# Masked attention: contiguous query operands, first scores between output projections, reciprocals through transposes, pieces in thirds, beginning reordered

## The reference

```python
x = x + _L0_xattn_ref(_layernorm(x, axis=-1), ctx_2048, mask_SxS2_bc0, mask_BxS2_bk0, ...)   # this one
x = x + _L0_ffn_ref(...)
x = x + _L1_xattn_ref(...)
x = x + _L1_ffn_ref(...)

def _L0_xattn_ref(X, encoder_output, causal_mask, padding_mask, Wq, bq, Wk, bk, Wv, bv, Wo, bo):
    q = X @ Wq.T + bq; k = encoder_output @ Wk.T + bk; v = encoder_output @ Wv.T + bv
    scores = einsum('bgrqd,bgkd->bgrqk', q, k) / sqrt(16)
    scores = where(causal_mask, -inf, scores); scores = where(padding_mask, -inf, scores)
    w = softmax(scores, axis=-1)
    return einsum('bgrqk,bgkd->bgrqd', w, v) (heads joined) @ Wo.T + bo
```

## Time and profile before

| | |
|---|---|
| time, median of 3 runs | 1809.57 us (1807.93 to 1809.96) |
| profiled execution | 1812.99 us, its span 1811.2 us |
| TensorE busy, over the span | 1500.2 us (83%) |
| VectorE, ScalarE, GpSimd busy | 862.8, 713.0, 396.9 us |
| masked attention | 0 to 653 us of the span |
| of it, before the first batch's weighing | 101 us |
| mean DMA rate over the span | 76 GB/s |

### The profile page before, as it was taken

One profiled execution on the slowest core, in us unless ns is written; L12 is line 12 of the kernel. 1 busy time (PEld: TensorE's weight loads), 2 busy tenths in 40 slices (PEclk: granted clock), 3 DMA queues, 4 the chain that ended last, 5 costly groups with the idle time before them and its releaser, 6 DMA issues. The chain is left out here.

```text
span 1811.2 us, 23713 instructions
## 1 busy us (share of the span) xinstructions
PE 1500.2 (83%) x9156; PEld 687.6 (38%) x9234; DVE 862.8 (48%) x1318; ACT 713.0 (39%) x1292; POOL 396.9 (22%) x479
## 2 busy tenths in 40 slices
PE   3568888778787827888936999999599999999998
PEld 2334444345344313444421222222244444444443
DVE  6444735548457327777525666663263131221220
ACT  2143444444434516777722655655243021120120
POOL 4300101101000016676541322321353000000000
PEclk8678889889888859999975999999699999999999
DMA  5524253351542220100025444420442200100100
GB/s 137 96 89 90 97 144 86 107 118 59 143 88 77 76 105 7 37 34 18 18 66 162 141 118 123 136 83 25 163 119 80 70 1 1 69 0 0 47 1 24
DMA packets 89546, 138.14 MB, mean 76 GB/s; under 512 B 7496, under 2 KB 48008, under 8 KB 88912
## 3 DMA queue, kind: packets, MB, share of 16 engines
q1 hardware_dynamic: 76640, 111.54, 22.3%
q10 hardware_dynamic: 12800, 25.17, 4.4%
HBM read 105.85 MB, written 30.83 MB: 75 GB/s over the span
## 5 line engine op out<-in xcount | busy, mean ns | idle before, releaser
L488 DVE TENSOR_REDUCE a_negmax<-a_psX 128x4 f32<-128x1024 f32 x128 | 149.9, 1218 | 173.0 <-PE a_psX L682 172.4
L1425 DVE TENSOR_REDUCE c_negmax<-c_psA 128x1 f32<-128x512 f32 x256 | 165.9, 683 | 99.4 <-PE c_psA L1489 98.0
L373 ACT ACTIVATE a_probs<-a_psB 128x512 f32<-128x512 f32 x256 | 138.5, 593 | 148.6 <-PE a_psB L692 148.4
L1790 PE MATMUL d_psGU<-d_zt_lo,d_w_hi 128*128 128x512 bf16 x501 | 191.7, 383 | 4.8 <-POOL d_w_lo L1673 4.3
L1790 PE MATMUL d_psGU<-d_zt_hi,d_w_hi 128*128 128x512 bf16 x502 | 191.8, 382 | 3.0 <-ACT d_silu L1710 2.4
L1790 PE MATMUL d_psGU<-d_zt_hi,d_w_lo 128*128 128x512 bf16 x501 | 191.6, 382 | 0.6
L1372 ACT ACTIVATE c_probs<-c_psB 128x512 f32<-128x512 f32 x256 | 140.2, 595 | 109.1 <-PE c_psB L1502 109.1
L692 PE MATMUL a_psB<-a_qs,a_ks 115*128 115x256 bf16 x512 | 138.7, 402 | 46.0 <-ACT a_probs L373 40.4
L1710 ACT ACTIVATE d_silu<-d_psGU 128x512 f32<-128x512 f32 x64 | 38.2, 596 | 350.5 <-PE d_psGU L1790 350.4
L1754 DVE TENSOR_TENSOR d_h<-d_psGU,d_silu 128x512 f32<-128x512 f32 x64 | 44.3, 692 | 226.4 <-PE d_psGU L1790 226.2
L1489 PE MATMUL c_psA<-c_ks,c_qs 96*128 96x512 bf16 x256 | 105.1, 413 | 41.9 <-DMA c_qs<-q_scr 28.3
(11 more groups left out here) (214 smaller groups left out, 2609.2 us busy)
## 6 DMA issues: line engine op xcount, KB each, us to landing
a_tern_stage<-in_w ACTq DMA_DIRECT2D x32, 768.0 KB, 7.8
d_weight_stage<-in_w_last SPq DMA_DIRECT2D x24, 512.0 KB, 4.0
a_ks<-k_scr SPq DMA_DIRECT2D x24, 256.0 KB
a_qs<-q_scr SPq DMA_DIRECT2D x24, 256.0 KB
c_ks<-k_scr SPq DMA_DIRECT2D x48, 128.0 KB, 2.6
c_qs<-q_scr SPq DMA_DIRECT2D x48, 128.0 KB, 3.0
a_xz<-in_x SPq DMA_DIRECT2D x8, 512.0 KB, 18.4
a_ctx<-in_ctx_t SPq DMA_DIRECT2D x8, 512.0 KB, 12.8
```

The lines of the kernel that those rows point to most:

```text
L373: act.activation(pr[:, e % 4, :, jj * P:(jj + 1) * P].rearrange("p r (a i) -> p a r i", a=2), B[:, u % 2, :].rearrange("p (a r i) -> p a r ...
L488: v.tensor_reduce(negm[:, u, :], X[:, 2 * (u % 2):2 * (u % 2) + 2, :].rearrange("p a (j k) -> p (a j) k", k=SEQ), AX.X, ALU.max, negate=Tr ...
L1425: v.tensor_reduce(negm[:, u:u + 1], A[:, u % 2, :], AX.X, ALU.max, negate=True)\
L1790: last = pe.matmul(GU[:, 2 * up + i % 2, :], wgu[wh][:, i, up, k, :], zt[zh][:, k, :], start=(k == 0 and j == 0), stop=(k == DC - 1 and j ...
```

## The change

All of it lies in `build_masked_attention` and in two weight layouts made on the host.

- Query operand: the tokens of a batch are loaded into `xz` in the order (j, i) by `rows`, two transfers for one; `wq` and `bq` are permuted on the host so that query chunk c holds head c of each group; `q_hi`, `q_lo`, `q_scr`, `qs`, `m_t` get layouts in which the 128 or 256 columns of one j are contiguous. Four transfers from `q_hi` and `q_lo` to `q_scr` take the place of eight.
- First scores: the four score units of group 0 of batch b + 1 are issued in `project`, two ahead of each half of the output projection of batch b, and their exponentials follow ScalarE's part of `project`.
- Reciprocals: ScalarE copies the weighed values and sums (`results`), TensorE transposes the sums (`turn_sums`), VectorE takes the reciprocals of 128 x 16 elements, GpSimd repeats each 16 times (`spread`), TensorE transposes back (`turn_recips`), VectorE multiplies. Multiplication and the halves follow one or two steps later than before.
- GpSimd's order for batch b: `inputs(b + 2)`, adding `bo`, `scales(b + 2)`, then four times `spread`. VectorE's statistics (`inputs(b + 2)`) move from step 4 to step 1, ScalarE's `normalise(b + 2)` from step 5 to step 6.
- Pieces: `piece` is cut into thirds, spread over the steps by `THIRDS`; the next load is issued behind the last third.
- `MAXES` starts at step 2.
- Beginning: `wo` is split after the second projection; the second batch's statistics and the mask constants stand inside the first projection.

Left out of the diff below: declarations, names of semaphores, and lines whose only change is a name, a count or a layout.

```diff
...
-    PIECE_AT = (0, 2, 4, 6)
-    TOTAL_AT = ROUNDS // len(PIECE_AT) - 1
-    MAXES = (0, 1, 2, 2, 2, 3, 3, 3)
+    PIECES = 4
+
+    THIRDS = (0, 2, 2, 1, 2, 2, 2, 1)
+    TOTAL_AT = ROUNDS // PIECES - 1
+    MAXES = (0, 0, 2, 2, 3, 3, 3, 3)
     with ExitStack() as ctx:
         sb = lambda name, shape, dt: ctx.enter_context(nc.sbuf_tensor(name, shape, dt))
...
+        os_sb = sb("a_out_sums", [P, 2, SEQ], F32)
+        r16 = sb("a_sums_recip", [P, ST, GROUPS], F32)
+        rb = sb("a_recip_rows", [P, ST, P], F32)
...
+        def thirds(b, g):
+
+            at = PIECES * 3 * b + sum(THIRDS[:g])
+            return [divmod(k, 3) for k in range(at, at + THIRDS[g])]
...
             def inputs(n):
                 need(sp, s["zt_done"], n)
-                sp.dma_start(xz[:], x_in[n * SEQ:(n + 1) * SEQ, :].rearrange("(t p) d -> p t d", p=P))\
-                    .then_inc(s["xz_loaded"], DMA)
+                for t in range(ST):
+                    sp.dma_start(xz[:, t, :], rows(x_in, n, t)).then_inc(s["xz_loaded"], DMA)
                 need(sp, s["ctx_split"], 2 * n)
...
                         sp.wait_ge(s[done], 2 * n + half + 1)
-                        for c in (2 * half, 2 * half + 1):
-                            sp.dma_start(io["q_scr"][part_of].rearrange("p (c h) t -> c h p t", c=DC)[c], q[:, c, :])\
-                                .then_inc(s["q_out"], DMA)
+                        sp.dma_start(io["q_scr"][part_of].rearrange("p g (c n) -> c g p n", c=2)[half],
+                                     q[:, half].rearrange("p j c i -> p (j c i)")).then_inc(s["q_out"], DMA)
...
+            def spread(b, c):
...
+                k = DC * b + c
+                pool.wait_ge(s["recip_done"], k + 1)
+                need(pool, s["recip_turned"], k)
+                g.tensor_copy(rb[:].rearrange("p t (n d) -> p (t n) d", d=HD),
+                              r16[:].rearrange("p t (n o) -> p (t n) o", o=1).broadcast_to([P, ST * GROUPS, HD]))\
+                    .then_inc(s["recip_spread"], 1)
...
             for b in range(BATCH):
                 if b + 2 < BATCH:
-                    scales(b + 2)
                     inputs(b + 2)
                 pool.wait_ge(s["c_loaded"], 5 * DMA)
                 pool.wait_ge(s["xr_loaded"], (b + 1) * ST * DMA)
                 for t in range(ST):
                     g.tensor_tensor(xr[:, t, :], xr[:, t, :], keep["bo"][:], ALU.add).then_inc(s["bo_added"], 1)
+                if b + 2 < BATCH:
+                    scales(b + 2)
+                for c in range(DC):
+                    spread(b, c)
...
+            def results(b, c):
+                act.wait_ge(s["pv_done"], GROUPS * b + 2 * c + 2)
+                need(act, s["o_norm"], DC * b + c)
+                act.activation(os_sb[:].rearrange("p a t -> p (a t)"), OS[:, c % 2].rearrange("p a t -> p (a t)"), ACT.Copy)\
+                    .then_inc(s["os_copied"], 1)
...
+            def copy_max(m):
+                act.wait_ge(s["mt_done"], m + 1)
+                need(act, s["mt_out"], m * DMA)
+                act.activation(m_t[:], X[0:2 * MU, 1, :].bitcast(BF16)[:, 0:QJ * P], ACT.Copy).then_inc(s["mt_copied"], 1)
...
             def project(n, m, b):
+                if b is not None:
+                    results(b, DC - 1)
...
                 if m is not None:
-                    act.wait_ge(s["mt_done"], m + 1)
-                    need(act, s["mt_out"], m * DMA)
-                    act.activation(m_t[:].rearrange("n h i j -> n j (h i)"),
-                                   X[0:2 * MU, 1, :].bitcast(BF16)[:, 0:QJ * P].rearrange("n (j q) -> n j q", j=QJ),
-                                   ACT.Copy).then_inc(s["mt_copied"], 1)
+                    copy_max(m)
                 if b is not None:
-                    out_high(b, DC - 1)
+                    out_high(b, DC - 2)
...
+                if b is not None:
+                    out_high(b, DC - 1)
+                if n == 0:
+                    normalise(1)
+                if n is not None:
+                    need(act, s["q_out"], n * 4 * DMA)
...
+            def third(r, j):
                 act.wait_ge(s["tern_loaded"], (r + 1) * DMA)
...
+                if j == 2:
+                    load_piece(r + 1)
...
             def attend(b):
-                for g in range(GROUPS):
+                for g in range(1, GROUPS):
+                    behind = thirds(b, g)
+                    if g in (3, 5, 7):
+                        results(b, (g - 3) // 2)
                     exponentials(b, 2 * g)
+                    for k in behind[:1]:
+                        third(*k)
                     exponentials(b, 2 * g + 1)
-                    if g in PIECE_AT:
-                        piece(piece_at(b, g))
-                    if g == 5 and b + 2 < BATCH:
+                    for k in behind[1:]:
+                        third(*k)
+                    if g == 6 and b + 2 < BATCH:
                         normalise(b + 2)
-                    if g in (3, 5, 7):
-                        out_high(b, (g - 3) // 2)
+                    if g in (5, 7):
+                        out_high(b, (g - 5) // 2)
...
             project(0, None, None)
-            normalise(1)
+            project(1, None, None)
             split_weight(3)
-            project(1, None, None)
-            act.wait_ge(s["mt_done"], 1)
-            act.activation(m_t[:].rearrange("n h i j -> n j (h i)"),
-                           X[0:2 * MU, 1, :].bitcast(BF16)[:, 0:QJ * P].rearrange("n (j q) -> n j q", j=QJ),
-                           ACT.Copy).then_inc(s["mt_copied"], 1)
+            copy_max(0)
+            exponentials(0, 0)
+            exponentials(0, 1)
             for b in range(BATCH):
                 attend(b)
                 project(b + 2 if b + 2 < BATCH else None, b + 1 if b + 1 < BATCH else None, b)
+                if b + 1 < BATCH:
+                    exponentials(b + 1, 0)
+                    exponentials(b + 1, 1)
...
+                if b is not None:
+                    normalise(b, DC - 1)
+                    out_low(b, DC - 1)
+                if n == 0:
+                    inputs(1)
+                    constants()
+                if n is not None:
+                    queries_low(n)
                 if b is not None:
                     dve.wait_ge(s["bo_added"], ST * (b + 1))
                     for t in range(ST):
@@ -508,17 +557,15 @@
                         for u in range(sum(MAXES[:g]), sum(MAXES[:g + 1])):
                             reduce_unit(b + 1, u)
                     if g in (2, 4, 6):
-                        c = g // 2 - 1
-                        reciprocals(b, c, 0)
-                        reciprocals(b, c, 1)
-                        normalise(b, c)
-                    if g == 4 and b + 2 < BATCH:
+                        reciprocals(b, g // 2 - 1)
+                    if g in (3, 5, 7):
+                        normalise(b, (g - 3) // 2)
+                    if g == 1 and b + 2 < BATCH:
                         inputs(b + 2)
-                    if g in (3, 5, 7):
-                        out_low(b, (g - 3) // 2)
-                    r = piece_at(b, g - 1)
-                    if r is not None and r >= ROUNDS:
-                        for j in range(3):
+                    if g in (5, 7):
+                        out_low(b, (g - 5) // 2)
+                    for r, j in thirds(b, g):
+                        if r >= ROUNDS:
...
+            def constants():
+                dve.wait_ge(s["constants"], 5)
...
-            split_weight(2)
-            dve.wait_ge(s["constants"], 5)
-            v.tensor_copy(ks[0][0:QI], mask_b.rearrange("p j (o k) -> p j o k", o=1)
-                          .broadcast_to([QI, QJ, GROUPS, SEQ])).then_inc(s["constants"], 1)
-            v.tensor_copy(qs[1][R_ONES:P].rearrange("p h (a n) -> p (h a) n", n=P), ones).then_inc(s["constants"], 1)
-            v.tensor_copy(ks[1][R_ONES:P].rearrange("p j g (a n) -> p (j g a) n", n=P), ones).then_inc(s["constants"], 1)
+            v.tensor_copy(qs[0][0:QI].rearrange("p h (j i) -> p (h j) i", i=QI),
+                          keep["ident_bf"][0:QI, 0:QI].rearrange("p (o i) -> p o i", o=1)
+                          .broadcast_to([QI, HEADS * QJ, QI])).then_inc(s["constants"], 1)
             project(0, None)
-            inputs(1)
-            split_weight(3)
             project(1, None)
             for u in range(MU):
                 reduce_unit(0, u)
             split_max(0)
+            split_weight(3)
             for b in range(BATCH):
                 attend(b)
                 project(b + 2 if b + 2 < BATCH else None, b)
...
+            def turn_sums(b, c):
+
+                pe.wait_ge(s["os_copied"], DC * b + c + 1)
+                for t in range(ST):
+                    last = pe.transpose(OS[:, c % 2, 1, t * P:(t + 1) * P], os_sb[:, 1, t * P:(t + 1) * P], keep["ident"][:])
+                last.then_inc(s["sums_turned"], 1)
+
```

(48 more changed lines are left out.)

133 lines of the change are left out of this document (66 added, 67 removed).

## The result

The changed kernel takes 1966.73 us (median of 4 runs, 1966.21 to 1967.08). The kernel before, run beside it, takes 1809.17 us. The ratio is 1.087 (95% interval 1.086 to 1.088): slower by 157 us. In the profiled execution the span is 1964.4 us against 1811.2, and all of the 153 us lie in the masked attention: the next layer's first load is issued at 807.32 us instead of 653.73.

What follows compares the result with a forecast made beforehand. TensorE, with the waits in its order, was taken to bound masked attention. 1812.99 + 113 (five batches) + 36 (last two) - 2 (beginning) = 1960, less 3.4 for the profiled execution: 1957 us, range 1895 to 2010.

Steps and rivals of the forecast that it cites:

- The two-engine queue: SyncE's transfers: stores, xz and xr share two DMA engines, about 11 us a pair; xz lands at 40, xr at 53.5.
- Stacks: Query stacks in a middle batch: land at 18 us instead of 19.3, thanks to four fewer DMA issues.
- GpSimd's part: After xr lands in a batch: adding bo 2.6 us, scales 1.6, spread 0.6; done at 58.4 with gaps.
- The tail: From spread done to the next zero: 37.2 us, including 4.1 in step 6 waiting for a weight piece.
- A batch: Each of five middle batches: 95.2 us against 72.55, so +113 us in all.
- The last two batches: End of attention: batch 6 takes 89.5 us against 69.8, batch 7 64.7 against 48.7; together +36.
- The beginning: Up to batch 0's output projection: 159 us instead of 161.46, so -2, between -10 and +10.
- A: Rival: xz doesn't queue with stores and xr, so xr lands at 43.5, a batch is 85 us: 1898; chance 0.08.
- B: Rival: score matmuls stay at 0.225 us because the operand's step is not what slows them: 1984; chance 0.10.
- C: Rival: piece waits fully exposed in steps 2, 4, 6, TensorE long at half clock: about 2020 us; chance 0.08.
- D: Rival: GpSimd has xr before TensorE needs the spread, no stall stays, 66 us a batch: 1762; chance 0.04.
- contiguous queries: Score matmul's moving operand: 0.11 us apiece instead of 0.225, 7.3 us per batch if TensorE is late.

Runs made afterwards that it cites:

- e1: Changed kernel with the xz loads, xr loads and output stores cut by partition halves, over 16 DMA engines: 1776.2 us, ratio 0.983 to the kernel before.
- e2: Changed kernel with only the xz loads cut by partition halves, over 16 engines; xr and stores unchanged: 1899.2 us, ratio 1.051 to the kernel before.
- e3: Changed kernel with only GpSimd's order changed, spread 0 and 1 first, ahead of adding bo; transfers stay on two engines: 1879.9 us, ratio 1.040.
- e7: Kernel before with only the xr loads and the stores cut by partition halves, over 16 engines: 1800.7 us, ratio 0.996.
- e4: e1 with the next weight piece's load issued behind the second third of the present piece, not the last: 1771.1 us, ratio 0.980.
- e6: e5 with the score matmul's moving operand again taken in steps of four elements: 1749.4 us, ratio 0.968 to the kernel before.
- e5: e4 with spread 0 and 1 ahead of adding bo in GpSimd's order and VectorE's statistics at step 3: 1722.9 us, ratio 0.953.
- e10: Kernel before with the score matmul taking 256 neighbouring columns of its moving operand, not every fourth: 1795.7 us, ratio 0.993.
- e12: e5 with the first group's four score units again behind the output projection, only TensorE's order changed: 1728.0 us, ratio 0.954.
- e9: e5 with VectorE's long reciprocals as in the kernel before, without copy, spread and transposes: 1731.1 us, ratio 0.956.
- e11: e5 with the query stacks read back in halves, six transfers for three, groups 4 to 7 on their own semaphore: 1702.6 us, ratio 0.941.

## Why the prediction was right

1957 was forecast, 1966.7 measured, inside the range, and by the mechanism named. Point by point, against the trace after, with offsets in the batch counted from its first scores at 163.73:

- **The two-engine queue.** Both links were where they were put, and e1, e2 and e3 show each by taking it away. `xz` was sized at 40 of the batch and landed at 44.5 (208.29 - 163.73); GpSimd had `xr` at 56.5 (forecast 53.5, with the context between). Each pair was taken at 11 us, and the pairs were put behind the stacks. From the landing of the stacks (184.97) to that of `xz` stores and `xz` took 23.3 us, forecast 22, and from there `xr` reached GpSimd after 11.9, forecast 13.5. So the size of the pairs was right to 2 us each time, and most of the 4.5 us by which `xz` was late is the stacks. The Trainium skill's rule ("DMA: Bandwidth & Descriptors", "Why a DMA increments its semaphore by 16 and not by 1"), weighed in the prediction, agrees with the 0.13 above and with what another cut of the same bytes gave in e1 and e7.
- **Stacks** landed at 21.2 and not 18 (19.3 before). Fewer issues on SyncE didn't bring them forward; why they came late stays open. TensorE's wait for them cost nothing, since VectorE's stall came after, but the forecast's queue starts at their landing, and there the 3.2 us appear.
- **GpSimd's part** was sized 2.6 + 1.6 + 0.6 and took 2.48 + 1.6 + 0.40: spread done at 61.0 (224.75), forecast 58.4.
- **The tail** from there was 37.2 and took 35.4 (224.8 to 260.18). The wait for a piece in step 6 was sized 4.1 us on the path. ScalarE waited 1.59 us (238.20), and TensorE not at all. That was the mis-sized term of this part, and e4 repeats it: an earlier load took 54 us of ScalarE's waits away and moved the end by 5. Steps 4 to 6 took 5.4 us each, not 5; in each TensorE waited 0.88 us for VectorE's three reductions, which were put at 0.5. That the batch came out right to 1 us is in part luck: the spread was 2.6 us late and the tail 1.8 us short.
- **A batch**: 95.9 us from 164.39 to 644.06, forecast 95.2: +117 for the five, where +113 stood. (The walk itself adds up to 95.6; the forecast took 0.4 off without a reason, and its bounds as written add up to 1894 and 2012, not 1900 and 2005.)
- **The last two batches**: 152.3 us in all (644.06 to 796.33, the end of the last sum) against 154.2. The forecast's 89.5 for batch 6 run to the end of its projection. There, at 734.08, the weighing of batch 7 begins, 90.0 us in; the rest took 62.3 where 64.7 stood. `xr` of batch 7 was at GpSimd 27.5 us behind that (761.59), forecast 28.4.

```profile
734.08 1.07 PE L774 MATMUL a_psOS<-a_probs,a_v 128*32 128x256 f32 x16
```

```profile
761.59 2.48 POOL L310 TENSOR_TENSOR a_xr<-a_xr,bo 128x512 f32<-128x512 f32 x2 [41.78 <-DMA a_xr<-in_x]
```

- **The beginning** was forecast at -2 and came out at +2.9 (output projection at 164.39 for 161.46). The two sides of that small sum were larger than they were put: 15 us lost to `xz` on two engines, not 9, and 18 gained by the new order ahead of the first scores. From there batch 0 took 5.8 us longer than before (66.7 for 60.9), with its own stall. That the sum came out near zero is luck.
- **The rivals.** A (`xz` not in the queue) is excluded by the wait at 208.29. B (score matmuls stay at 0.225) is refuted by 229.60 to 230.05 and by e6, and with it, for a moving operand in steps of four two-byte elements, the rule of the Trainium skill ("SBUF — State Buffer", "Door 1: The DMA port swizzle"), as it was weighed in the prediction. C fell with the wait for a piece. D was right that without the stall the change is faster, but not in its size. With the transfers alone mended (e1) GpSimd no longer waits for `xr`, and a batch takes 70.9 us and not D's 66, since the context and the stacks hold it: 1776 and not 1762. With the orders mended too (e5) it is 1723, because then no spread but the last two stands behind `xr`.

What the prediction valued too high was the gain left without the stall. It gave contiguous queries 7.3 us a batch "if TensorE is what is late" and the first scores 3. Contiguous queries measured 2.7 us a batch in the kernel before (e10) and 3.8 in e5 (e6), the first scores 2.1 (e12, from one profile each and not clear of the noise), the reciprocals 1.6 (e9, where 7.4 us of VectorE had gone). Those of e5 sum to 7.5 of the 10.4 us by which its batches are shorter than the old ones. How the rest divides between the removed wait for scales, the maxima that start at step 2 and the overlap of all these was not measured.

## What to carry to other kernels

Before moving an operation in an in-order queue, ask when the data of everything ahead of it lands, not how long it runs. Here a 0.4 us copy put behind an addition that waits for a load, and a reduction put behind another load, left TensorE waiting 30 us in a batch. Look at the DMA share while a transfer runs alone; 0.13 says that two engines carry it, and cutting the same bytes along a long axis gave back 190 us. And time saved ahead of a fixed arrival is paid back as waiting: shorten the arrival first (e11), then the work.

## What had not been expected of the hardware

An issue on SyncE itself blocked when it stood behind transfers on two engines, whatever its own form. In the changed kernel the two `xz` transfers held its queue 15.56 us, the context's next to them 7.41, `xr` 6.74. But e2's `xz`, which goes over 16 engines, took 10.62 us to issue behind the stores on two; the plain `xz` of the kernel before took 6.48, and 0.69 in e7, where only stores and `xr` have another form. In e5 `xz` took 2.08.

```profile
153.75 10.62 SPq L177 DMA_DIRECT2D a_xz<-in_x  x2
```

```profile
245.94 0.69 SPq L171 DMA_DIRECT2D a_xz<-in_x  x1
```

The context, itself a plain transfer, came late in the changed kernel: GpSimd began on it 45 us after the start of the output projection (209.60), in e5 28 us after (222.61). What fills up and blocks the queue, the traces don't show.

And the clock fell with the waits: 0.77 granted in the changed kernel's batch, 0.88 before, 0.97 in e5. It stood at 0.50 from 202 to 218, while TensorE mostly waited. Right behind the stall, still at 0.50, 16 weighing matmuls took 1.7 us from start to start (226.27 to 227.98), and 0.9 us at a granted clock of 1.00 from 233.17. So a stall also lengthens the work just behind it.
